# The projection of a wavelet mix as two half-height products per pair of nodes, in place of one block-diagonal product

## The reference

```python
sig = x.transpose(0, 2, 3, 1).reshape(-1, T)
a = sig
for _ in range(3):
    a, d = _dwt(a)
    details.append(d)
enh = [c * w[i] for i, c in enumerate([a] + details[::-1])]   # w: one weight per channel
rec = enh[0]
for d in enh[1:]:
    rec = _idwt(rec[:, :d.shape[-1]], d)
xr = rec.reshape(B, N, D, T).transpose(0, 3, 1, 2)
return x + xr @ proj_w.T + proj_b
```

## Time and profile before

| | us |
|---|---|
| median of 2 runs | 2706.96 (2705.8 to 2708.12) |
| profiled execution, its span | 2706.9 |
| PE matmul busy | 2597.5 (96%) |
| PE weight load busy | 2566.6 (95%) |
| DVE busy | 2263.8 (84%) |
| ACT busy | 682.8 (25%) |
| mean granted TensorE clock | 0.983 |

### The profile page before, as it was taken

One profiled execution on the slowest core, in us unless ns is written; L12 is line 12 of the kernel. 1 busy time (PEld: TensorE's weight loads), 2 busy tenths in 40 slices (PEclk: granted clock), 3 DMA queues, 4 the chain that ended last, 5 costly groups with the idle time before them and its releaser, 6 DMA issues.

```text
span 2706.9 us, 63231 instructions
## 1 busy us (share of the span) xinstructions
PE 2597.5 (96%) x20700; PEld 2566.6 (95%) x20700; DVE 2263.8 (84%) x6908; ACT 682.8 (25%) x1387; POOL 6.5 (0%) x52
## 2 busy tenths in 40 slices
PE   7999999999999999999999999999999999999998
PEld 7999999999999999999999999999999999999998
DVE  5887888788788878878887887888888788788887
ACT  2222222222222222222222222222222222222222
POOL 0000000000000000000000000000000000000000
PEclk9999999999999999999999999999999999999999
DMA  6766767667676766767676676766666676677674
GB/s 147 174 167 155 171 156 175 151 167 167 158 168 157 174 152 160 174 155 168 162 175 144 168 173 153 171 161 162 156 171 166 153 177 160 145 175 167 168 175 107
DMA packets 199991, 438.85 MB, mean 162 GB/s; under 512 B 11240, under 2 KB 11241, under 8 KB 199657
## 3 DMA queue, kind: packets, MB, share of 16 engines
q1 hardware_dynamic: 199088, 434.15, 66.9%
q10 hardware_dynamic: 569, 0.14, 0.0%
HBM read 217.20 MB, written 217.06 MB: 160 GB/s over the span
## 4 chain that ended last, share of the span: by engine, by line
PE 95%; issue 3%; DVE 1%; ACT 0%; DMA 0%; ACTq 0%
PE coefs_ps L279 35%; PE proj_ps L298 34%; PE synth_ps L309 9%; PE synth_ps L310 9%; PE synth_ps L311 9%; DVE proj_lo L444 0%; DMA bias_sb<-bias 0%; ACT proj_hi L391 0%; ACT proj_hi L376 0%; DVE proj_lo L408 0%; ACTq L364 0%; ACTq L368 0%; DVE x_sb L453 0%; ACTq L365 0%; DVE coefs_sb L425 0%
## 5 line engine op out<-in xcount | busy, mean ns | idle before, releaser
L298 PE MATMUL proj_ps<-w_sb,coefs_sb 128*124 128x128 f32 x8280 | 1145.9, 274 | 81.8 <-issue 81.5
L298 PEld LDWEIGHTS proj_ps<-w_sb,coefs_sb 128*124 128x124 f32 x8280 | 1095.0, 188 | 94.9 <-issue 87.1
L391 ACT ACTIVATE proj_hi<-proj_ps 124x384 fp32r<-124x384 f32 x1380 | 679.1, 492 | 1997.6 <-PE proj_ps L298 1997.6
L279 PE MATMUL coefs_ps<-analysis_sb,x_sb 104*128 104x124 f32 x8280 | 1076.7, 278 | 17.7 <-DMA analysis_sb<-analysis_m 12.1
L444 DVE TENSOR_TENSOR proj_lo<-proj_ps,proj_hi 124x384 fp32r<-124x384 f32 x1380 | 770.0, 558 | 376.7 <-ACT proj_hi L391 367.3
L279 PEld LDWEIGHTS coefs_ps<-analysis_sb,x_sb 104*128 104x128 f32 x8280 | 1025.6, 195 | 22.1 <-DMA analysis_sb<-analysis_m 12.1
L453 DVE TENSOR_TENSOR x_sb<-synth_ps,x_sb 104x384 f32<-104x384 f32 (+1 forms) x1380 | 757.1, 549 | 0.5 <-PE synth_ps L311 0.5
L309 PE MATMUL synth_ps<-proj_hi,synthesis_lo 125*104 125x384 f32 (+1 forms) x1380 | 581.1, 421 | 0.5 <-DVE x_sb L453 0.4
L310 PE MATMUL synth_ps<-proj_lo,synthesis_hi 125*104 125x384 f32 (+1 forms) x1380 | 467.3, 339 | 0.0
L311 PE MATMUL synth_ps<-proj_hi,synthesis_hi 125*104 125x384 f32 (+1 forms) x1380 | 466.7, 338 | 0.0
L425 DVE TENSOR_TENSOR coefs_sb<-coefs_ps,scale_sb 128x312 f32<-128x312 f32 x828 | 391.9, 473 | 4.4 <-issue 4.4
(11 more groups left out here) (8 smaller groups left out, 4.4 us busy)
## 6 DMA issues: line engine op xcount, KB each, us to landing
x_sb<-x SPq DMA_DIRECT2D x184, 936.0 KB
out<-x_sb SPq DMA_DIRECT2D x184, 936.0 KB
x_sb<-x SPq DMA_DIRECT2D x184, 216.0 KB
out<-x_sb SPq DMA_DIRECT2D x184, 216.0 KB
synthesis_sb<-synthesis_m ACTq DMA_DIRECT2D x1, 50.8 KB
analysis_sb<-analysis_m ACTq DMA_DIRECT2D x1, 50.4 KB
comp_sb<-comp_w ACTq DMA_DIRECT2D x2, 1.0 KB, 7.6
w_sb<-w_t ACTq DMA_DIRECT2D x2, 16.0 KB, 10.0
```

Of the source, the lines that this page charges most:

```text
L279: mm = nc.tensor.matmul(coefs_ps[local % 2][:, part, at:at + COLS], x_sb[s][0:rows(w), w, col:col + PAIR], analysis_sb[0:rows(w), :], star ...
L298: mm = nc.tensor.matmul(proj_ps[local % 2][0:COLS, p * PAIR:(p + 1) * PAIR], coefs[:, at:at + COLS], w_sb[:, :], start=True, stop=True)
L391: nc.scalar.activation(proj_hi[w][0:COLS, :], proj_ps[local % 2][0:COLS, 0:GROUP], ACT.Copy).then_inc(hi_copied, 1)
```

## The change

The projection of a pair becomes two products, one per node. Node 0's has the coefficients' partitions 0 to 63 as its stationary operand (64 x 124), node 1's the partitions 64 to 127; the moving operand is the same 64 x 64 weight, which lies twice in `w_sb`, now 128 x 64, once on each half of the partitions. Node 0 of each of the three pairs writes the first bank of `proj_ps`, node 1 the second, 192 columns in each. So a window takes both banks, where windows took turns before, and `project` waits for the split of the window before it (`lo_copied` at `done * WINDOWS + w`) and not of the one before that. ScalarE's copy and VectorE's split read both banks in one instruction and write in the old order of nodes (a view with the node as an axis of its own). `w_sb` is no longer cleared, and ScalarE waits for one memset only.

```diff
--- before.py
+++ after.py
@@ -152,7 +152,7 @@
         synthesis_sb = sb("synthesis_sb", [COLS + 1, WINDOW])
         synthesis_hi = sb("synthesis_hi", [COLS + 1, WINDOW], fp32r)
         synthesis_lo = sb("synthesis_lo", [COLS + 1, WINDOW], fp32r)
-        w_sb = sb("w_sb", [PAIR, PAIR])
+        w_sb = sb("w_sb", [PAIR, CHANNELS])
         comp_sb = sb("comp_sb", [PAIR, COMPONENTS])
         scale_sb = sb("scale_sb", [PAIR, ALL_COLS])
         bias_sb = sb("bias_sb", [COLS + 1, GROUP])
@@ -162,7 +162,7 @@
         proj_lo = [sb(f"proj_lo{w}", [COLS + 1, GROUP], fp32r) for w in range(WINDOWS)]
 
         coefs_ps = [pb(f"coefs_ps{i}", [PAIR, 2, 512]) for i in range(2)]
-        proj_ps = [pb(f"proj_ps{i}", [128, 512]) for i in range(2)]
+        proj_ps = pb("proj_ps", [128, 2, 512])
         synth_ps = [pb(f"synth_ps{i}", [128, 512]) for i in range(2)]
 
         cleared = sem("cleared")
@@ -188,6 +188,14 @@
         UNIT_DMAS = 4
         GROUPS_PER_TURN = SLOTS * GROUPS
 
+        def by_node(ap):
+
+            return ap.rearrange("c (p two e) -> c two p e", two=2, e=CHANNELS)
+
+        def projected_rows(m):
+
+            return proj_ps[0:m, :, 0:GROUP // 2].rearrange("c two (p e) -> c two p e", e=CHANNELS)
+
         def rows(w):
             return WINDOW if w < FULL_WINDOWS else LAST
 
@@ -286,17 +294,19 @@
             def project(turn, s, g, w, first):
                 done = turn * GROUPS_PER_TURN + s * GROUPS + g
                 local = (s * GROUPS + g) * WINDOWS + w
-                if not (first and local < 2):
-
-                    pe.wait_ge(lo_copied, done * WINDOWS + (w - 1))
+                if not (first and local < 1):
+
+                    pe.wait_ge(lo_copied, done * WINDOWS + w)
                 for p in range(PAIRS):
                     if w == 0:
 
                         pe.wait_ge(scaled, done * PAIRS + p + 1)
                     coefs = coefs_sb[((s * GROUPS + g) * PAIRS + p) % COEF_BUFS]
                     at = first_col(w)
-                    mm = nc.tensor.matmul(proj_ps[local % 2][0:COLS, p * PAIR:(p + 1) * PAIR],
-                                          coefs[:, at:at + COLS], w_sb[:, :], start=True, stop=True)
+                    for node in range(2):
+                        half = slice(node * CHANNELS, (node + 1) * CHANNELS)
+                        mm = nc.tensor.matmul(proj_ps[0:COLS, node, p * CHANNELS:(p + 1) * CHANNELS],
+                                              coefs[half, at:at + COLS], w_sb[half, :], start=True, stop=True)
                 mm.then_inc(projected, 1)
 
             def synthesise(turn, s, g, w, first):
@@ -363,9 +373,9 @@
             for half in halves:
                 act.dma_start(comp_sb[half, :], comp_w).then_inc(comp_loaded, 16)
             act.dma_start(analysis_sb[:, :], analysis_m).then_inc(analysis_loaded, 16)
-            act.wait_ge(cleared, 2)
+            act.wait_ge(cleared, 1)
             for half in halves:
-                act.dma_start(w_sb[half, half], w_t).then_inc(w_loaded, 16)
+                act.dma_start(w_sb[half, :], w_t).then_inc(w_loaded, 16)
             act.dma_start(synthesis_sb[:, :], synthesis_m).then_inc(consts_loaded, 16)
             act.dma_start(bias_sb[COLS:COLS + 1, :], bias).then_inc(consts_loaded, 16)
             act.wait_ge(consts_loaded, CONSTS_LOADED)
@@ -388,7 +398,7 @@
                             if not (first and local < WINDOWS):
 
                                 act.wait_ge(synthesised, done + (w + 1 - WINDOWS))
-                            nc.scalar.activation(proj_hi[w][0:COLS, :], proj_ps[local % 2][0:COLS, 0:GROUP],
+                            nc.scalar.activation(by_node(proj_hi[w][0:COLS, :]), projected_rows(COLS),
                                                  ACT.Copy).then_inc(hi_copied, 1)
 
             turn_of(0, first=True)
@@ -397,7 +407,6 @@
 
         @block.vector
         def _(dve):
-            nc.vector.memset(w_sb[:, :], 0.0).then_inc(cleared, 1)
             nc.vector.memset(bias_sb[:, :], 0.0).then_inc(cleared, 1)
 
             dve.wait_ge(hi_built, 1)
@@ -438,11 +447,9 @@
             def split_low(turn, s, g, w):
 
                 done = (turn * GROUPS_PER_TURN + s * GROUPS + g) * WINDOWS
-                local = (s * GROUPS + g) * WINDOWS + w
-
                 dve.wait_ge(hi_copied, done + (w + 1))
-                nc.vector.tensor_tensor(proj_lo[w][0:COLS, :], proj_ps[local % 2][0:COLS, 0:GROUP],
-                                        proj_hi[w][0:COLS, :].bitcast(fp32), ALU.subtract).then_inc(lo_copied, 1)
+                nc.vector.tensor_tensor(by_node(proj_lo[w][0:COLS, :]), projected_rows(COLS),
+                                        by_node(proj_hi[w][0:COLS, :].bitcast(fp32)), ALU.subtract).then_inc(lo_copied, 1)
 
             def add_window(turn, s, g, w):
```

## The result

The changed kernel takes 3557.24 us (median of two, 3547.13 to 3567.34) against 2706.96: the ratio is 1.316, 95% interval 1.309 to 1.322. The profiled execution took 3567.34 us, its span is 3565.4. The forecast was 3521.

A forecast was written before the change was run, and what follows sets the result against it. TensorE bounds the kernel end to end, 9.25 us a group; two standstills of 0.91 and six changes of 0.20 add 3.02, times 276 is 834, less 20 at loop edges: 2707 + 834 - 20 = 3521 us, range 3100 to 4600.

The forecast's parts named there:

- What bounds the kernel: Whole kernel: TensorE is the chain from end to end, 9.25 us a group; the load sets the pace within it.
- P: TensorE's projection of one window: six records at 110 ns, 0.66 us before the change.
- The argument from 111 against 110 ns: Analysis against projection records: more columns loaded, fewer streamed, yet 111 against 110 ns; a stream-set pace would give 107.
- Part 1: Projection as two half-height products: loads of the halves run side by side, so P stays 0.66 us.
- Part 2: One buffer for two: projections 3 and 0 wait for the previous window's split, standstills of 0.91 us twice a group.
- Part 3: Changes between full and half height around projections: ten a group, six not hidden, 0.20 us each, 1.20 us a group.
- The clock: Rival for TensorE throughout: idle 15% or more of each group, it gets half clock, 5200 us; chance 0.06, wholly or partly.
- sign of a wrong whole: The forecast is wrong if standstills are missing or the granted clock falls under 0.9 in the steady slices.
- Part 4: Kernel start: one memset of 0.165 us and a wait go, but a bias DMA of 11.8 us rules; gain nothing.

The follow-up runs named there:

- the third order: Changed kernel with TensorE and VectorE steps reordered: synthesis 3 behind analysis 1, 4 and 0 behind project 2, 1 and 2 behind project 4; 3597.53 and 3675.16 us.

## Why the prediction was right

- **What bounds the kernel, and that the load sets P.** Shown to within 0.04 us of P: 104 ns a load with 12 full-height loads in a row, next to no change with half the stream, 0.83 ns a column less with fewer columns. The argument from 111 against 110 ns in the earlier trace rows was thin but pointed the right way.
- **Part 1, P at 0.66 with loads side by side.** Right, with a size a little off: 12 records take 0.63 us, if entering half height costs the 0.19 us here that it cost alone. That is 5 x 0.03 = 0.15 us a group in favour of the change. The reason given was separate rows and separate banks. It needs the alternating order as well (1.07 us against 0.82 without it), which the prediction didn't see.
- **Part 2, two standstills.** Right in place, number and mechanism: 533 waits (552 less those at loop edges), and 1.24 and 1.16 us from a projection's end to the next one's start, where 1.20 + 0.04 was worked out. The restart was 0.26 where 0.19 was taken, seen alone with the wait only: standstills of 0.98 and 0.90 us, where 0.91 was taken for each. In the changed kernel this restart and the entry into half height are one thing: the projection behind a standstill takes 0.86 us, 0.04 more than any other, so entering half height there hides in the restart, as was forecast.
- **Part 3, changes of height.** Right: 0.19 us to enter, 0.17 to 0.20 to leave, where 0.20 was taken from a range of 0 to 0.35. That this value came so near is partly luck. Put together from the chain: the five projections are 4.16 us against 3.30 (0.86 more; forecast 2 x 0.19 + 3 x 0.20 = 0.98), the three exits that are not hidden 0.57 (forecast 0.60), and the two waits 1.24 + 1.16 less two syntheses of 0.52 are 1.36 (forecast 1.44). That makes 9.25 + 2.79 = 12.04, of 12.03 in the chain; 12.27 was predicted.
- **The clock.** The step that was off. The rival said that TensorE, idle a part of each group, might be granted half the clock for good, at 5200 us; the forecast priced the clock at nothing. It came in part, 113 us, and not by the idle share: with only the wait, TensorE was busy for 86% of the span, least of all, and had the clock of the kernel before (0.984). With the halves in a row or 32 columns it was busy for 97 to 98% and had the lowest clocks (0.547 and 0.564). The prediction's own sign of a wrong whole, a granted clock under 0.9 in the steady slices, is there on the page: nine of the 40 slices read 8 or 7. Away from the stretches behind the loop's edges the clock is full (1.00 in 360 to 480 us), so the sign was badly chosen, since a slice of 89 us can't tell the two. But pricing the clock at nothing was wrong. Predicted time plus this, less 0.24 us x 276 = 66 for the group, plus 10 for a smaller gain at the edges: 3521 + 113 - 66 + 10 = 3578, of 3567 in the profiled execution. Two errors of opposite sign, a group 66 us too dear in all and a clock 113 us too cheap, made the forecast look closer (1%) than its steps were; that part is luck.
- **Part 4.** The first projection starts at 24.2 us against 24.7: nothing, as said.

## What to carry to other kernels

Half-height products save stream time, and a kernel whose pace is set by loading the stationary operand has next to none to save (here 0.03 of 0.66 us): count loads times stationary columns first, and moving columns second. Price each alternation between products of different height (here 0.19 us each way), and look at what the two halves' separate banks take away: here the second buffer, worth 19% by itself. Where a single buffer can't be avoided, the chain from producer through all readers and back (here 1.24 us) has to be covered by work in every gap, not on average.

## What the runs showed of the hardware

- **Loads on the two halves of the array run side by side, if the products alternate**: 12 in 0.63 us against 1.25 at full height, and about 0.88 when one half's products stand in a row. The 0.63 and 0.88 are 0.82 and 1.07 less 0.19 for entering half height. The two halves wrote two banks throughout, so whether the banks must differ too was not tried. The Trainium skill's "TensorEngine Tiling (Array Packing)", Tiling Modes, says that tiles load and multiply in parallel; this case agrees, best where the halves alternate.
- **A change of height costs TensorE about 0.19 us each way**, with nothing waited for and no second half beside it: six records 0.85 us against 0.66, and the next analysis 1.31 against 1.11.
- **A load takes 0.83 ns a column at full clock and 1.7 ns at 1.2 GHz**, from 28 columns fewer in six loads (0.14 and 0.28 us).
- **Once at 1.2 GHz, TensorE can stay there longer, and it does so most with half-height products.** In the kernels of this study with a clock of 0.84 and more, each stretch at 1.2 GHz began at the start, at a loop edge, where TensorE had stood still for 2 to 7 us, or at the end. At edges they lasted 3.4 to 6.8 us in the kernel before, and the same with only the wait. They lasted up to 31 us with full-height products of 64 columns (mean clock 0.970), so half height is not needed for it; up to 37 in the changed kernel, up to 72, once, with one half-height product a pair (0.970), and up to 150 in the third order (0.840). With the halves in a row (0.547) or 32 moving columns (0.564), 1.2 GHz also came back between edges and took most of the span. What the clock goes by was not settled.
- **A loop's edge costs about 5.9 us in this kernel** (14 of them gave 82 us): some 4 us of standstill and the half clock behind it.
